# When x is loaded, and when the first scores start: a two-layer graph attention kernel

## The reference

```python
def layer(x, W, adj):                    # called for two weights in turn
    Wh, Ws = split(x @ W, 2, axis=-1)    # 4096 x 256 each
    scores = Wh @ Ws.T                   # 4096 x 4096
    a = softmax(scores, axis=-1) * adj
    return leaky_relu(a @ Wh + x, 0.01)

y = layer(layer(x, W[0], adj), W[1], adj)
out = layernorm(x + y, axis=-1)          # eps 1e-5
```

## Time and profile before

| | us |
|---|---|
| median of 3 runs | 1616.54 (1615.24 to 1624.44) |
| profiled execution, its own time | 1615.16 |
| its span in the trace | 1613.3 |
| granted TensorE clock, mean | 0.992 |
| PE busy | 1564.4 (97%) |
| DVE busy | 1335.7 (83%) |
| POOL busy | 813.4 (50%) |
| ACT busy | 647.4 (40%) |

### The profile page before, as it was taken

The page is one execution under the profiler, slowest core; times in us unless marked ns, Lnnn a source line. Parts: engine busy times, 40 slices in busy tenths (PEclk is TensorE's granted clock), DMA queues, the critical chain, the costliest instruction groups (busy, mean ns, idle before and its releaser), DMA issues.

```text
span 1613.3 us, 23318 instructions
## 1 busy us (share of the span) xinstructions
PE 1564.4 (97%) x8104; PEld 1325.2 (82%) x8104; DVE 1335.7 (83%) x1558; ACT 647.4 (40%) x1175; POOL 813.4 (50%) x807
## 2 busy tenths in 40 slices
PE   7999999999999999999799999999999999999996
PEld 6888888888888888887688888888888888888874
DVE  4688778877887788778737899999999999999994
ACT  4344444444444444444333444444344444443441
POOL 0055555555555555555511555555555555555555
PEclk9999999999999999999999999999999999999999
DMA  5277767777767777779914777777777777767784
GB/s 189 63 190 191 197 187 201 186 201 188 201 189 200 186 200 186 202 188 228 257 48 107 197 192 211 195 203 190 204 197 206 192 211 194 203 191 204 197 213 116
DMA packets 167748, 302.57 MB, mean 188 GB/s; under 512 B 39760, under 2 KB 68432, under 8 KB 167504
## 3 DMA queue, kind: packets, MB, share of 16 engines
q1 hardware_dynamic: 105808, 132.75, 32.8%
q0 software_dynamic: 36864, 134.23, 29.5%
q10 hardware_dynamic: 24960, 34.11, 7.9%
HBM read 157.29 MB, written 9.44 MB: 103 GB/s over the span
## 4 chain that ended last, share of the span: by engine, by line
PE 90%; DVE 3%; DMA 2%; ACT 1%; POOL 1%; issue 1%; SPq 1%; ACTq 1%; POOLq 0%
PE banks L507 28%; PE banks L396 16%; PE banks L398 16%; PE banks L397 16%; PE banks L509 14%; POOL a_lo L847 1%; DVE ring L743 1%; SPq L287 1%; DMA turned<-ring 1%; DVE ring L748 1%; DVE neg_max L715 1%; ACTq L287 1%; PE banks L438 0%; DMA load<-adj 0%; DVE x_t L679 0%
## 5 line engine op out<-in xcount | busy, mean ns | idle before, releaser
L847 POOL TENSOR_TENSOR a_lo<-turned,a_hi 128x512 fp32r<-128x512 f32 x512 | 660.3, 1304 | 653.1 <-ACT a_hi L625 651.3
L507 PE MATMUL banks<-wh,a_hi 128*128 128x512 f32 x2048 | 741.1, 401 | 23.9 <-POOL a_lo L847 23.8
L607 ACT ACTIVATE ring<-banks,neg_max 128x1024 f32<-128x1024 f32 x256 | 286.1, 1118 | 856.6 <-DVE neg_max L715 845.6
L509 PE MATMUL banks<-wh,a_lo 128*128 128x256 f32 x2048 | 577.9, 282 | 0.0
L507 PEld LDWEIGHTS banks<-wh,a_hi 128*128 128x128 f32 x2048 | 388.5, 190 | 122.5 <-POOL a_lo L847 20.2
L715 DVE TENSOR_REDUCE neg_max<-banks 128x1 f32<-128x1024 f32 x256 | 312.1, 1219 | 164.4 <-PE banks L398 164.4
L396 PE MATMUL banks<-x_t,q_t 128*128 128x512 f32 x1024 | 408.0, 398 | 6.8 <-DVE q_t L679 6.8
L398 PE MATMUL banks<-x_t,q_t 128*128 128x512 f32 x1024 | 403.4, 394 | 0.0
L397 PE MATMUL banks<-x_t,q_t 128*128 128x512 f32 x1024 | 401.2, 392 | 0.0
L509 PEld LDWEIGHTS banks<-wh,a_lo 128*128 128x128 f32 x2048 | 389.9, 190 | 8.0
L743 DVE SCALAR_TENSOR_TENSOR ring<-ring,weight,load 128x1024 f32<-128x1024 f32 x256 | 329.2, 1286 | 6.3 <-DMA load<-adj 6.2
(11 more groups left out here) (60 smaller groups left out, 757.6 us busy)
## 6 DMA issues: line engine op xcount, KB each, us to landing
load<-adj POOLq DMA_DIRECT2D x256, 512.0 KB, 5.1
turned<-ring SPq DMA_DIRECT2D x1528, 64.0 KB, 4.0
turned<-ring ACTq DMA_DIRECT2D x520, 64.0 KB, 3.3
ring<-x SPq DMA_DIRECT2D x8, 512.0 KB, 5.8
rows<-x SPq DMA_DIRECT2D x32, 128.0 KB, 3.3
x_scratch<-rows SPq DMA_DIRECT2D x32, 128.0 KB, 3.0
rows<-x_scratch SPq DMA_DIRECT2D x32, 128.0 KB, 3.4
first_rows<-x SPq DMA_DIRECT2D x32, 128.0 KB, 3.2
```

Source lines behind the costliest of these rows:

```text
L507: nc.tensor.matmul(psum[:, bank, :], a_hi[:, s, b], wh[:, k].rearrange("p a d -> p (a d)"), start=start, stop=stop, skip_group_check=True)
L509: last = nc.tensor.matmul(psum[:, bank, 0:D], a_lo[:, s, b], wh[:, k, 0], start=False, stop=stop, skip_group_check=True)
L607: nc.scalar.activation(ring_at(i).rearrange("p (r b j) -> p b r j", r=2, j=QUAD), psum[:, 2 * (i % 2):2 * (i % 2) + 2, :].rearrange("p h ( ...
L847: nc.gpsimd.tensor_tensor(a_lo[:, j % 2].rearrange("p b (r j) -> p b r j", r=QUADS), as_f32(turned[:, unit % 2, :, b:b + SUB, :]).rearrang ...
```

## The change

x's first seven groups are loaded at once, into seven different places; the eighth follows when layer 0's raw weight was read, and the second weight when five groups were transposed. The first score starts after six transposed groups. Groups 6 and 7, the transposes of the second weight and its M are put behind scores 0, 1 and 2 (`head_at`). The second weight's M waits in the last quarter of `wh` instead of in `load`. In both layers wh sides are made two a step, in steps 0 to 7 and in steps 4 to 7. x's groups use three pairs of banks instead of two, and layer 0's first eight wh sides use two banks instead of four. The cut diff; left out are the bank names' use in the splits, the same reordering on VectorE, and the number of semaphores:

```diff
--- before.py
+++ after.py
@@ -92,12 +92,21 @@
         w_made = [[w_part[:, part] for part in range(2)],
-                  [load[:, part].bitcast(F32R).rearrange("p (k e) -> p k e", k=KT) for part in range(2)]]
+                  [wh[:, TILES - 4 + 2 * part:TILES - 2 + 2 * part].rearrange("p b a d -> p (b a d)")
+                   .rearrange("p (k e) -> p k e", k=KT) for part in range(2)]]
+        wt_banks = [psum[:, bank:bank + 2, :] for bank in (SIDE_BANK, ACC_BANK)]
+        m_banks = [psum[:, bank, :] for bank in (SIDE_BANK + 1, ACC_BANK)]
+        FIRST_BANKS = [0, 2, 6, 0, 2, 6, 2, 6]
+        FIRST_FREE = [0, 0, 0, 1, 2, 3, 5, 6]
...
@@ -217,8 +226,12 @@
+        def head_at(step):
+            return {0: [("x", 6), ("x", 7)], 1: [("wt", 1)], 2: [("w", 1)]}.get(step, [])
         EARLY = WPAIRS // 2
-        WH_AFTER = [{0: 3, 1: 3, 2: 3, 3: 3, 4: 2, 5: 2}, {3: 3, 4: 3, 5: 2}]
+        WH_AFTER = [{n: 2 for n in range(8)}, {n: 2 for n in range(4, 8)}]
@@ -250,7 +263,7 @@
             kind, n = s
-            wide = kind == "wh" and (n < WPAIRS or n >= WPAIRS + EARLY)
+            wide = kind == "wh" and n % WPAIRS >= EARLY
             side_bank[s] = min(range(SIDE_BANK, SIDE_BANK + (4 if wide else 2)),
@@ -258,11 +271,11 @@
-        x_rows = [ring[:, g % 4, :] for g in range(GROUPS)]
+        x_rows = [ring[:, n, :] for n in (0, 1, 2, 3, 5)] + [load[:, 0, :], load[:, 1, :], ring[:, W_SLOT, :]]
         x_rows += [as_f32(q_t[:, p]).rearrange("p a k n -> p (a k n)") for p in range(2)]
...
         x_rows += [ring_at(X_CHUNK[14]), ring_at(X_CHUNK[15])]
-        x_place = [g % 4 for g in range(GROUPS)] + [4, 5, 6, 7, 4, 5, 8, 9]
+        x_place = list(range(GROUPS)) + [8, 9, 10, 11, 8, 9, 12, 13]
@@ -345,15 +358,15 @@
             load_w(0)
-            for g in range(2):
+            for g in range(GROUPS - 1):
                 load_x(g)
+            sp.wait_ge(wt_done, 1)
+            sp.wait_ge(w_lo, 1)
+            load_x(GROUPS - 1)
+            sp.wait_ge(xt_done, 5)
             load_w(1)
-            for g in range(2, 4):
-                load_x(g)
-            for g in range(4, GROUPS):
-                sp.wait_ge(xt_done, g - 3)
-                load_x(g)
             for t in range(2):
@@ -403,7 +416,7 @@
                         at = (b % 2 * KT + kt) * P
-                        last = nc.tensor.transpose(psum[:, SIDE_BANK + b // 2, at:at + P],
+                        last = nc.tensor.transpose(wt_banks[layer][:, b // 2, at:at + P],
                                                    w_rows[layer][:, kt, b * P:(b + 1) * P], ident[:])
...
@@ -431,8 +444,8 @@
                     pe.wait_ge(xt_lo, X_FREE[g])
-                elif 2 <= g < GROUPS:
-                    pe.wait_ge(xt_lo, g - 1)
+                elif g < GROUPS and FIRST_FREE[g]:
+                    pe.wait_ge(xt_lo, FIRST_FREE[g])
                 for kt in range(KT):
@@ -452,7 +465,7 @@
                         else:
-                            pe.wait_ge(w_lo, 4)
+                            pe.wait_ge(w_lo, 2)
                     for dt in range(KT):
@@ -464,6 +477,9 @@
                         pe.wait_ge(xt_lo, layer * GROUPS + (half + 1) * GROUPS // 2)
+                    if not layer and bank >= ACC_BANK:
+                        pe.wait_ge(w_lo, 4)
                     if layer and bank >= ACC_BANK:
@@ -479,8 +495,8 @@
                 if t == 0:
-                    pe.wait_ge(xt_lo, layer * GROUPS + 2 * c + 2 if layer == 0 or c == CPT - 1
-                               else layer * GROUPS + GROUPS - 1)
+                    pe.wait_ge(xt_lo, [4, 7, 7, 8][c] if layer == 0 else layer * GROUPS + GROUPS - (c < CPT - 1))
                 if c == 0 and t % 2 == 0:
@@ -515,16 +531,10 @@
-            pe.wait_ge(wt_lo, 1)
-            transpose_w(1)
             transpose_x(2)
-            make_m(1)
-            for g in range(3, GROUPS):
+            make_side(("q", 0))
+            for g in range(3, 6):
                 transpose_x(g)
-            pe.wait_ge(wt_lo, 2)
-            make_side(("q", 0))
             for step in range(STEPS):
@@ -542,6 +552,15 @@
                     scores(i)
+                for kind, n in head_at(step):
+                    if kind == "x":
+                        transpose_x(n)
+                    elif kind == "wt":
+                        pe.wait_ge(xt_lo, GROUPS)
+                        transpose_w(n)
+                    else:
+                        make_m(n)
                 for side in sides_after(step):
...
@@ -585,6 +604,9 @@
                         act.wait_ge(product_done, SUBS)
+                    if n == WPAIRS - 2:
+                        act.wait_ge(w_next_stored, 32)
                     j = 2 * (n % WPAIRS)
@@ -602,7 +624,11 @@
                             act.wait_ge(xt_done, g + 1)
-                elif W_SLOT <= i % RING < W_SLOT + LAYERS:
+                elif i < 4:
+                    act.wait_ge(xt_done, i + 1)
+                elif i < W_SLOT + LAYERS:
+                    act.wait_ge(xt_done, GROUPS)
                     act.wait_ge(w_lo, 4)
@@ -636,12 +662,10 @@
             split_x(1)
-            split_wt(1)
             split_x(2)
-            split_w(1)
-            for g in range(3, GROUPS):
+            split_side(("q", 0))
+            for g in range(3, 6):
                 split_x(g)
-            split_side(("q", 0))
             for step in range(STEPS):
@@ -670,6 +694,8 @@
                     exponentials(i)
+                for kind, n in head_at(step):
+                    {"x": split_x, "wt": split_wt, "w": split_w}[kind](n)
                 for side in sides_after(step):
...
@@ -854,9 +880,9 @@
-            pool.wait_ge(w_next_stored, 32)
             for i in range(2):
+                pool.wait_ge(xt_done, GROUPS - 2 + i)
                 load_adj(nc.gpsimd, i)
```

More of the change, by code:

```diff
@@ L125, in gat_layernorm @@
         w_next_stored, w_next_loaded = sem("w_next_stored"), sem("w_next_loaded")
-        x_loaded = [sem(f"x_loaded{s}") for s in range(10)]
+        x_loaded = [sem(f"x_loaded{s}") for s in range(14)]
         xt_done, xt_hi, xt_lo = sem("xt_done"), sem("xt_hi"), sem("xt_lo")
@@ L413, in make_m @@
                     last = three_products(
-                        psum[:, ACC_BANK + layer, ct * D:(ct + 1) * D],
+                        m_banks[layer][:, ct * D:(ct + 1) * D],
                         [(w_t[layer][0][:, 0, et * D + ct * P:et * D + (ct + 1) * P],
@@ L421, in transpose_x @@
             def transpose_x(g):
-                pair = X_BANKS[g] if g >= GROUPS else 2 * (g % 2)
+                pair = X_BANKS[g] if g >= GROUPS else FIRST_BANKS[g]
                 pe.wait_ge(x_loaded[x_place[g]], x_count(g))
@@ L555, in split_wt @@
                 act.wait_ge(wt_done, layer + 1)
-                nc.scalar.activation(w_t[layer][0], psum[:, SIDE_BANK:SIDE_BANK + 2, :], ACT.Copy).then_inc(wt_hi, 1)
+                nc.scalar.activation(w_t[layer][0], wt_banks[layer], ACT.Copy).then_inc(wt_hi, 1)
             def split_w(layer):
@@ L562, in split_w @@
                 nc.scalar.activation(w_made[layer][0][:, :, D:2 * D],
-                                     psum[:, ACC_BANK + layer, :].rearrange("p (k e) -> p k e", k=KT),
+                                     m_banks[layer].rearrange("p (k e) -> p k e", k=KT),
                                      ACT.Copy).then_inc(w_hi, 1)
             def split_x(g):
-                pair = X_BANKS[g] if g >= GROUPS else 2 * (g % 2)
+                pair = X_BANKS[g] if g >= GROUPS else FIRST_BANKS[g]
                 act.wait_ge(xt_done, g + 1)
@@ L682, in split_wt @@
                 dve.wait_ge(wt_hi, layer + 1)
-                low(w_t[layer][1], psum[:, SIDE_BANK:SIDE_BANK + 2, :], w_t[layer][0]).then_inc(wt_lo, 1)
+                low(w_t[layer][1], wt_banks[layer], w_t[layer][0]).then_inc(wt_lo, 1)
             def split_w(layer):
@@ L689, in split_w @@
                 dve.wait_ge(w_hi, 2 * layer + 2)
-                low(w_made[layer][1][:, :, D:2 * D], psum[:, ACC_BANK + layer, :].rearrange("p (k e) -> p k e", k=KT),
+                low(w_made[layer][1][:, :, D:2 * D], m_banks[layer].rearrange("p (k e) -> p k e", k=KT),
                     w_made[layer][0][:, :, D:2 * D]).then_inc(w_lo, 1)
             def split_x(g):
-                pair = X_BANKS[g] if g >= GROUPS else 2 * (g % 2)
+                pair = X_BANKS[g] if g >= GROUPS else FIRST_BANKS[g]
                 dve.wait_ge(xt_hi, g + 1)
```

## The result

The changed kernel takes 1613.86 us in the median of 20 runs (1610.14 to 1618.62), the kernel before 1618.34 (1614.88 to 1624.44) in as many. The ratio is 0.9972, 95% interval 0.9962 to 0.9982: 4.5 us faster, 2.9 to 6.2.

A forecast was written before the change was run, and what follows sets the result against it. TensorE, fully busy from 84 to 740 us, left only gaps before the products. Layer 0's 4.2 gained less layer 1's 2.5 lost gave 1.7: 1615.16 to 1613.5 profiled, put at 1614.0 between two readings; range 1609 to 1618.5.

The forecast's parts named there:

- Score 0 at 19.6: Head of layer 0: the first score starts at 19.6 us, 10.4 earlier than before.
- Moved work 4.7, steps 5.62, new waits nothing: Layer 0, scores 0 to 4: work put behind scores adds 4.7 us, each TensorE step takes 5.62, new waits cost nothing.
- Rings of 6.66, 6.64, 8.4: Steps 5 to 7: VectorE and ScalarE wait for each other between maxima, about 6.6, 6.6 and 8.4 us against TensorE's 5.62.
- Rival (b): Both layers' starts: VectorE and ScalarE keep up, TensorE runs through; 10.5 + 4.3 us gained, 1600.4; chance 0.05.
- Product 0 5.7 after maximum 7: Layer 0, end of step 7: maximum 7 at 71.5 us, product 0 at 77.2, against 83.88 before.
- The term that was off: VectorE's step 8, ahead of product 2: weigh and turn 2.5 us, row sums 2.0, meeting a_lo 0.4.
- rival (c): Hole ahead of product 2: row sums take 0.8 instead of 2.0 us; 4.95 gained in all, 1610.2; chance 0.25.
- Layer 0: forecast 4.2: Layer 0 up to product 2: 4.65 us gained, less 0.4 for weigh meeting a_lo, gives 4.2.
- Layer 1: forecast 2.5 lost: Layer 1's start, its wh pairs moved to steps 4 to 7: loses 2.2 us plus 0.4, 2.5 in all.
- The border between the layers: From layer 0's product 2 on to layer 1: the lead won is carried, with no term for a change.
- The loads: Early loads of x in the head: costed at nothing; at most 2.3 us each, the eighth landing at 18.4.
- Rival (d): Steps 5 to 7, six rings in both layers: longer than forecast; 2.5 us slower, 1617.7 (at worst 1622); chance 0.17.

The follow-up runs named there:

- the one with the ring open: Changed kernel with, from step 4 on, the low parts of a step's wh pairs made behind the next step's weigh and turn: 1602.88 us.
- layer 1's new pairs alone: Kernel before with only layer 1's wh pairs placed two a step in its steps 4 to 7: 1619.69 us, ratio 1.0006.

## Why the prediction was right, and where it was off

The time, 1613.86, was forecast as 1614.0, the direction and the mechanism held; the gain was forecast as 1.7 and is 4.5, with an interval of 2.9 to 6.2 that leaves 1.7 out. That the time agrees to 0.14 us is luck: the kernel before has a median of 1618.34 in 20 runs, 1.8 above the one of three runs that the forecast stood on, and a gain taken 2.8 too small made up for a start taken too low.

- *Score 0 at 19.6*: 19.30 with the clock's late rise, on which the forecast's rows were taken. The early rise gives 17.40; it helps both kernels by 1.9 to 2.1, so it belongs to neither.
- *Moved work 4.7, steps 5.62, new waits nothing*: maximum 4 follows score 0 by 29.99 (forecast 30.2). TensorE waited once in between, 0.12 us for a low part of x.
- *Rings of 6.66, 6.64, 8.4*: 6.67, 6.63, 8.23. In layer 1 6.66, 6.63, 8.28. Rival (b), TensorE alone, was wrong for this kernel and right for the one with the ring open.
- *Product 0 5.7 after maximum 7*: 5.43.
- *The term that was off*, in both layers: step 8 on VectorE, from the last wh low to maximum 8, was 2.5 for weigh and turn, 2.0 for the row sums and 0.4 for meeting a_lo, 4.9. This term was mis-sized; it took 4.1 (73.09 to 77.17): weigh(3) did wait beside a_lo (2.20, +0.9), but the row sums behind it, 76.49 to 77.17, took 0.7 and not 2.0, because GpSimd was done by then. That is rival (c)'s mechanism, and its price (4.95 in all) came nearest to the 4.5. Layer 0: forecast 4.2, measured 5.5 (5.1 to 5.6); 0.8 of the 1.3 is this term, 0.3 the head, 0.2 to 0.4 the shorter last ring. Layer 1: forecast 2.5 lost, measured 1.1 against the old placement's median: the same 0.8, 0.2 the last ring, and 0.4 because the rows before came from an execution in which the transfers had not been late.
- *The border between the layers* was taken as rigid. No run shows that the change moves it, but it scatters by up to 5.9 us from one profile to the next.
- *The loads* cost nothing, as forecast, and at least those of groups 4 to 6 at once are worth nothing. The last of the seven landed at 15.6, where the bound of 2.3 us a load had 18.4.
- Rival (d), longer rings, did not happen: six rings within 0.2 us of the forecast's.

The Trainium skill, page GPSIMD Engine Reference, section Specifications, says that GpSimd shares its SBUF interfaces with VectorE, with contention for VectorE instructions that have two SBUF inputs or run in a 2-port perf mode. The trace agrees: beside a_lo weigh (two such inputs) takes 2.20 instead of 1.27, the first instruction of the row sums 0.85 against 0.12 without.

## What to carry to other kernels

When work at the start is moved forward, count the ring that the next stage closes: if VectorE must wait for ScalarE's answer before its own next item, the step costs the sum of both, not the larger (here 6.65 us, where TensorE's own step is 5.62), and a head start drains away in it. Letting the engine take its independent items first (here weigh and turn ahead of the wh lows) was worth 11 us, more than twice the change studied. A gain of a few us cannot be read from one pair of profiles: follow a landmark through several, and compare executions with the same clock.

## What the runs showed that I had not expected

TensorE's granted clock column reads 1.00 over the whole head, yet its matmuls there run at the lower level until 9.2 us in seven profiles and until 13.5 to 14.1 in four, whatever the kernel: 12 matmuls of 256 columns begin 0.12 or 0.21 us apart. It moves everything behind by 1.9 to 2.1 us.

In the hole ahead of product 0 the clock does fall in the column: in the kernel before it is 0.77 of full speed from 76.6 to 83.9, and the matmuls of score 8, behind 2.58 us of idleness, begin 0.43 apart instead of 0.23. The changed kernel has 1.00 in its own hole there (69.00 to 82.40). That could be taken for a part of the gain, but it cost nothing in layer 0: product 0 waits 0.28 us for a_lo all the same. In the profile of layer 1's new pairs alone the clock stayed at 1.00 there, and product 0 was ready only 0.4 earlier, because chunk 0's blocks had landed sooner.

And loads of the same 0.5 MB that stand on the chain between the layers took 5.2 to 8.6 us from issue to landing.
